# Null key and null value folded into keys and values by a context column, in a two-layer gated cross-attention kernel

## The reference

```python
x = layer_norm(x, g_norm)
q = x @ Wq
kv = context @ Wkv
k, v = jnp.split(kv, 2, axis=-1)
q, k, v = (to_heads(q), to_heads(k), to_heads(v))
nk = jnp.broadcast_to(null_kv[0], (b, HEADS, 1, DIM_HEAD))
nv = jnp.broadcast_to(null_kv[1], (b, HEADS, 1, DIM_HEAD))
k = jnp.concatenate([nk, k], axis=2)
v = jnp.concatenate([nv, v], axis=2)
...
attn = jax.nn.softmax(sim.astype(jnp.float32), axis=-1).astype(sim.dtype)
out = jnp.einsum('bhij,bhjd->bhid', attn, v)
out = out.transpose(0, 2, 1, 3).reshape(b, -1, INNER)
out = out @ Wout
return layer_norm(out, g_out)
```

## Time and profile before

| what | value |
|---|---|
| median of 3 runs | 330.18 us (328.82 to 331.27) |
| profiled execution | 329.04 us, of it 327.2 us span |
| TensorE busy (weight loads) | 92% (75%) |
| VectorE, ScalarE, GpSimd busy | 74%, 70%, 53% |

### The profile page before, as it was taken

One profiled execution on the slowest core, in us unless ns is written; L12 is line 12 of the kernel. 1 busy time (PEld: TensorE's weight loads), 2 busy tenths in 40 slices (PEclk: granted clock), 3 DMA queues, 4 the chain that ended last, 5 costly groups with the idle time before them and its releaser, 6 DMA issues.

```text
span 327.2 us, 7975 instructions
## 1 busy us (share of the span) xinstructions
PE 301.6 (92%) x2682; PEld 245.2 (75%) x2682; DVE 240.8 (74%) x723; ACT 230.5 (70%) x781; POOL 173.9 (53%) x301
## 2 busy tenths in 40 slices
PE   6779999999999869999999999999999998977595
PEld 6557668686767658898998988989888777743375
DVE  3887999999885456666777787777777686547865
ACT  2776596969899677877878778787787774319190
POOL 3115616252443145458889797895957849245100
PEclk9999999999999999999999999999999999979989
DMA  5671010002020000000000000000000000000004
GB/s 148 164 205 26 1 26 1 1 2 66 3 62 3 0 0 2 2 2 2 2 3 2 1 4 2 2 0 3 3 2 1 2 3 1 2 0 1 2 0 130
DMA packets 12649, 7.22 MB, mean 22 GB/s; under 512 B 3969, under 2 KB 12161, under 8 KB 12609
## 3 DMA queue, kind: packets, MB, share of 16 engines
q1 hardware_dynamic: 11728, 6.51, 7.2%
q10 hardware_dynamic: 880, 0.20, 0.3%
HBM read 5.66 MB, written 1.05 MB: 20 GB/s over the span
## 4 chain that ended last, share of the span: by engine, by line
PE 73%; DVE 8%; issue 7%; ACT 7%; POOL 4%; DVEq 0%; POOLq 0%; ACTq 0%
PE psum L1084 14%; PE psum L1220 10%; PE psum L1517 9%; PE psum L1531 7%; PE psum L1088 7%; PE psum L1090 6%; PE psum L1089 6%; PE psum L1099 2%; ACT work L1025 2%; DVE hgm L2149 2%; PE psum L1632 2%; PE psum L1540 1%; PE psum L1095 1%; DVE work L2008 1%; PE psum L1317 1%
## 5 line engine op out<-in xcount | busy, mean ns | idle before, releaser
L1025 ACT ACTIVATE work<-psum,nmx 128x129 f32<-128x129 f32 x256 | 83.4, 420 | 25.9 <-DVE nmx L2014 24.8
L603 POOL TENSOR_TENSOR work<-work,rden 128x512 f32<-128x512 f32 x64 | 66.4, 1038 | 0.0
L2014 DVE TENSOR_REDUCE nmx<-psum 128x4 f32<-128x516 f32 x64 | 41.5, 689 | 29.4 <-PE psum L1220 29.3
L1084 PE MATMUL psum<-ident,work 128*128 128x128 f32 (+2 forms) x376 | 58.4, 281 | 3.9 <-DVE work L2008 2.6
L1025 ACT ACTIVATION_READ_ACCUMULATOR work<-psum,nmx 128x1 f32 x256 | 58.7, 229 | 0.0
L1088 PE MATMUL psum<-split 128*128 128x256 f32 (+2 forms) x128 | 52.0, 406 | 1.5 <-issue 0.8
L1084 PEld LDWEIGHTS psum<-ident,work 128*128 128x128 f32 (+2 forms) x376 | 41.7, 142 | 13.1 <-issue 3.3
L2008 DVE COPY work<-psum 128x512 f32<-128x512 f32 x64 | 43.9, 686 | 7.8 <-PE psum L1084 4.9
L1090 PE MATMUL psum<-split 128*128 128x256 f32 (+2 forms) x128 | 43.3, 338 | 0.0
L1089 PE MATMUL psum<-split 128*128 128x256 f32 (+2 forms) x128 | 43.2, 338 | 0.0
L1220 PE MATMUL psum<-KT,work 64*128 64x129 f32 x512 | 37.5, 285 | 2.5 <-DVE den L2024 1.8
(11 more groups left out here) (209 smaller groups left out, 576.6 us busy)
## 6 DMA issues: line engine op xcount, KB each, us to landing
KT<-in_L_xattn_Wkv SPq DMA_DIRECT2D x2, 384.0 KB, 5.2
X<-in_x SPq DMA_DIRECT2D x1, 768.0 KB, 6.8
out_x<-X SPq DMA_DIRECT2D x3, 256.0 KB, 2.3
work<-in_ctx SPq DMA_DIRECT2D x3, 192.0 KB, 2.6
KT<-in_L_xattn_Wout SPq DMA_DIRECT2D x1, 512.0 KB, 4.7
work<-in_L_xattn_Wq SPq DMA_DIRECT2D x1, 512.0 KB, 3.6
work<-in_L_xattn_Wout SPq DMA_DIRECT2D x1, 512.0 KB, 4.0
X<-in_x SPq DMA_DIRECT2D x1, 256.0 KB, 3.3
```

Of the source, the lines that this page charges most:

```text
L603: pool.tensor_tensor(sx_[:, :, 0:S], sx_[:, :, 0:S], bcast(rden[n % 2][:, :], S), ALU.mult).then_inc(p_ready.sem, 1)
L1025: ins = act.activation(Sx[n % 4][:, j, :], psum[:, here, (j // 2) * K1:(j // 2 + 1) * K1], ACT.Exp, bias=nmx[n % 2][:, j:j + 1], accum_out ...
L1084: return pe.transpose(dst, src, ident[0:m, 0:m])
L2014: dve.tensor_reduce(nmx[n % 2][:, :].rearrange("p (c a) -> p c a", a=2), sim, AX_X, ALU.max, negate=True).then_inc(max_done.sem, 1)
```

## The change

The 97th column of the masked context is now minus the mask in place of the inverted mask, and the null value becomes a 97th row of the value weights, as the null key is one of the key weights. So an open position gets its key less the null key and its value less the null value, and a masked one gets zeros. Taking the null key off every key takes the same number off every logit of a row, so the softmax stays; the null logit is 0 and its key column is filled with zeros. The probabilities, the null one included, add up to 1, so the output is the product with the reduced values plus the null value, which ScalarE adds as a bias column while it copies the output (`oT`). What falls away: `pnr`, `pnT`, `nw`, `nvb`, the null transposes and products, their copies on ScalarE and VectorE and GpSimd's multiplication L601, the early load of the output weights (the later one, `ld_wo2`, stays) and the two loads of the null key as a column. There is one new small load, of 16 pieces of 256 bytes, in SP's queue right behind the value weights.

```diff
             load(wkv_f[1][0:CD, :], wkv[:, INNER:2 * INNER], ld_wv)
+            load(wkv_f[1][CD:CD + 1, :].rearrange("p (h e) -> p h e", h=NH),
+                 null_kv[1:2, :].rearrange("o (h e) -> o h e", h=1).to_broadcast([1, NH, DH]), ld_wv)
...
-            load(nk_col[0:DH, :], nk, ld_small)
-            load(nk_col[DH:P, :], nk, ld_small)
...
-            load(wo_f, wo_v, ld_wo)
...
-                pool.tensor_scalar(nvb, nvb, nv_col, None, ALU.mult).then_inc(setup_p.sem, 1)
...
-                pool.tensor_copy(KTb[:, :, :, S:K1].rearrange("p c b o -> p c (b o)"),
-                                 ones_of).then_inc(null_keys.sem, 1)
+                pool.memset(KTb[:, :, :, S:K1], 0.0).then_inc(null_keys.sem, 1)
...
-                pool.tensor_copy(cm_g[:, :, CD:CD + 1].rearrange("p b o -> p (b o)"),
-                                 not_mcol[:, s * G:(s + 1) * G]).then_inc(cm_done.sem, 1)
+                pool.tensor_scalar(cm_g[:, :, CD:CD + 1].rearrange("p b o -> p (b o)"), mcol[:, s * G:(s + 1) * G], -1.0,
+                                   None, ALU.mult).then_inc(cm_done.sem, 1)
...
-                if n % UPT < 2 and t >= 2:
-                    pool.wait_ge(pnt_done.sem, pnt_done.at(t - 1))
-                pool.tensor_tensor(pnr[t % 2][:, b % 2, HPU * hg:HPU * hg + HPU], sx_[:, :, S], rden[n % 2][:, :],
-                                   ALU.mult).then_inc(pnr_done.sem, 1)
...
-                act.activation(oT, bank[5], ACT.Copy).then_inc(ot_out.sem, 1)
...
-                act.activation(pnT[0:NH, :], bank[7][0:NH, 2 * S:4 * S], ACT.Copy).then_inc(pnt_out.sem, 1)
+                act.activation(oT, bank[5], ACT.Identity, bias=nv_col[:, 0:1]).then_inc(ot_out.sem, 1)
...
-                    ins = pe.matmul(bank[4][0:NH, 0:D], nvb[:, c, :], wo_f[:, c, :], start=(c == 0),
-                                    stop=(c == NCH - 1))
...
-                    ins = product3(dst, hi[0:CD, tk], lo[0:CD, tk], wkv_hi[0:CD, w], wkv_lo[0:CD, w])
+                    ins = product3(dst, hi[0:CD + 1, tk], lo[0:CD + 1, tk], wkv_hi[0:CD + 1, w], wkv_lo[0:CD + 1, w])
...
-                    ins = pe.matmul(bank[7][0:NH, (2 + bb) * S:(3 + bb) * S], pnr[t % 2][:, bb, :], ident[:, :],
-                                    start=False, stop=False, skip_group_check=True)
...
-                    ins = pe.matmul(bank[7][:, bb * D:(bb + 1) * D], pnT[:, bb * S:(bb + 1) * S], nw[:, :],
-                                    start=False, stop=False, skip_group_check=True)
...
-                dve.tensor_copy(nw[0:NH, :], bank[4][0:NH, 0:D]).then_inc(setup_v.sem, 1)
...
-                    dve.wait_ge(pnr_done.sem, pnr_done.at(n - 1))
```

More of the change, by code:

```diff
@@ L71, in flamingo_kernel @@
     I1P = NC1 * P
-    SMALL_LOADS = 10
+    SMALL_LOADS = 8
     W1_LOADS = 5
-    SETUP_V = 18
+    SETUP_V = 17
     ATT_SCALE = float(DH) ** -0.5
@@ L177, in flamingo_kernel @@
         oT = work.carve(4 * S)
-        pnT = work.carve(2 * S)
         yS = work.carve(2 * D).rearrange("p (b d) -> p b d", b=2)
@@ L261, in flamingo_kernel @@
         rden = [sb(f"rden{n}", [P, HPU]) for n in range(2)]
-        pnr = [sb(f"pnr{n}", [P, 2, NH]) for n in range(2)]
         sty, stx = (sb(n, [P, 2, 6]) for n in ("sty", "stx"))
@@ L280, in flamingo_kernel @@
         sig = signal
-        ld_mask, ld_bias, ld_small, ld_l0, ld_w0, ld_x0, ld_x, ld_wq, ld_wk, ld_wv, ld_w1, ld_wo = (
-            sig("ld_" + n) for n in ("mask", "bias", "small", "l0", "w0", "x0", "x", "wq", "wk", "wv", "w1", "wo"))
+        ld_mask, ld_bias, ld_small, ld_l0, ld_w0, ld_x0, ld_x, ld_wq, ld_wk, ld_wv, ld_w1 = (
+            sig("ld_" + n) for n in ("mask", "bias", "small", "l0", "w0", "x0", "x", "wq", "wk", "wv", "w1"))
         ctx_loaded = sig("ctx_loaded", 16, start=0)
@@ L712, in split_wkv @@
             def split_wkv(n):
-                rows = CD + 1 - n
+                rows = CD + 1
                 if n == 0:
@@ L1034, in _ @@
                     exponents(2 * (m - 1) + 1)
-                t = pair_at(m, PNT_AT)
-                if t is not None:
-                    pn_evac(t)
                 t = pair_at(m, Y_AT)
@@ L1131, in int8_transposes, with down_scale_out @@
                 ins.then_inc(setup_t.sem, 1)
[L1133 to L1141 removed]
+            def down_scale_out():
                 pe.wait_ge(setup_a.sem, setup_a.at(8))
@@ L1367, in _ @@
             kv(10)
-            null_values_out()
+            down_scale_out()
             text_proj(1)
@@ L1565, in _ @@
                     ins.then_inc(q_done.sem, 1)
-                t = pair_at(m, NULL_AT)
-                if t is not None:
-                    null_out(t)
                 if in_rounds(m - WO_LAG):
@@ L1574, in _ @@
                     out_proj(m - WO_LAG, 1)
-                t = pair_at(m, PNT_AT)
-                if t is not None:
-                    null_transposes(t)
                 if in_rounds(m - T_LAG):
@@ L1658, in split_wkv @@
             def split_wkv(n):
-                rows, cols = CD + 1 - n, slice(n * INNER, (n + 1) * INNER)
+                rows, cols = CD + 1, slice(n * INNER, (n + 1) * INNER)
                 dve.wait_ge(wkv_hi_done.sem, wkv_hi_done.at(n + 1))
```

66 lines of the change are left out of this document (11 added, 55 removed).

## The result

| | before | after |
|---|---|---|
| median | 330.73 us (4 runs, 328.82 to 331.57) | 320.87 us (4 runs, 319.21 to 325.35) |
| ratio, with its 95% interval | | 0.9687 (0.9642 to 0.9732) |
| profiled execution, span | 329.04, 327.2 us | 321.48, 319.6 us |

Three of the four times after lie between 319.21 and 321.48 us; the ratio leaves out the fourth, a disturbed run. The forecast was 321.8 us, in a range from 318.8 to 325.0 us.

A forecast was written before the change was run, and what follows sets the result against it. TensorE bounds the kernel (73% of the span), with a 2.80 us floor it doesn't set in each round's first piece. 3.7 + 2.1 + 0.6 + 2.0 = 8.4 us off 330.18 gives 321.8 us, range 318.8 to 325.0.

The forecast's parts named there:

- The null transposes: Attention rounds, TensorE's own piece: removing them saves their whole 0.53 us in seven rounds, 3.7 us.
- The null products: Attention rounds, first piece with a 2.80 us floor: removal saves 0.35 us in six full rounds, 2.1 us; the seventh nothing.
- the round with the collision: One traced round of 5.12 us, 0.28 over ordinary, where VectorE's normalisation took 1.09 us just after GpSimd's multiplication began.
- ScalarE's copy: Output copy in the rounds: the bias adds 0.07 us, bounds 0 and 0.14, covered by 0.78 us idle before the exponents.
- The end: After the last scores: GpSimd's multiplication 0.15 us and eighth null transposes 0.54 go, biased copy adds 0.07; together 0.6 us.
- The start: Before the text product: TensorE's waits, null products of the weights and a GpSimd step go; 2.0 us, bounds 0.97 and 2.9.
- the lower bound: For the start's gain: at least TensorE's two waits, for the masked context and for GpSimd's power, 0.97 us.
- Rival 1: Start gives nothing much: VectorE's chain or later weights hold the text product, TensorE's freed time becomes a wait; 323.3 us, chance 0.12.
- Rival 2: Attention rounds: GpSimd's long multiplication starts earlier and shuts out VectorE's normalisation, costing 5 x 0.28 us; 323.2 us, chance 0.08.
- Rival 3: Attention rounds: another loop holds the 4.84 us period, so only start and end count; 327.6 us, chance 0.06.
- Rival 4: Attention rounds: the granted clock falls to 1.2 GHz, two such rounds costing 9.7 us; 331.5 us, chance 0.04.

The follow-up runs named there:

- experiment 1: Changed kernel with two fp32 products of the null transposes' shape put back before the values in rounds 5, 9, ..., result unused; 324.04 us.
- experiment 2: Changed kernel with two unused fp32 products 128x128x128 put back before the first output products in rounds 6, 10, ...; 321.66 us.
- experiment 5: Changed kernel with ScalarE's output copy as a plain Copy again, leaving the null value out of the output; 320.50 us.
- experiment 6: Changed kernel with GpSimd's small 128x4 multiplication back ahead of the long one in all 64 units, result unused; 320.58 us.
- experiment 9: Changed kernel with the early output-weight load, eight weight products on TensorE and a 128x128 GpSimd multiplication put back, results unused; 320.72 us.
- experiment 4: Changed kernel with the early 512 KB output-weight load and eight fp32 products on those weights on TensorE put back, result unused; 321.88 us.
- experiment 3: Changed kernel with the early 512 KB load of the output weights back ahead of x in SP's queue, read by nobody; 319.92 us.
- experiment 10: Changed kernel with only a 128x128 GpSimd multiplication by a column put back ahead of the power of group 1; 319.46 us.
- experiment 7: Changed kernel with two one-column copies on VectorE ahead of the first normalisation of each pair, to start it later; 320.98 us.
- experiment 8: Changed kernel with 9 and 19 more clock-keeping products ahead of the two global maxima; 320.84 us median of 4 runs, ratio 0.9651.
- experiment 11: Changed kernel with the null value row's load moved behind the layer 0 weights and clock-keeping products at 45 and 39; 320.29 us median, ratio 0.9677.
- experiment 12: The kernel before, unchanged, run and profiled once more; 330.85 us.

## Why the prediction was right

**The null transposes (3.7 us).** Right, mechanism and size. Seven rounds went from 5.37 to 4.84 us, and experiment 1 brought 3.79 us back with TensorE's part alone.

**The null products (2.1 us).** Right: six rounds from 5.19 to 4.84, the seventh unchanged, and experiment 2 brings 0.36 us back six times and nothing the seventh time. Reading the period against the ordinary round, rather than adding up the 0.60 us of the removed matmuls, gave the number: six times 0.60 would have been 3.6 us. The sum leaves 6.24 less 3.8 less 2.1, about 0.3 us, and that is the round with the collision, which the forecast did not count as a gain.

**ScalarE's copy.** Its cover held. Its price, 91 ns, is over the 70 ns taken and under the bound of 140. A nearer row than the two tiles of half the width was there, and I overlooked it: the kernel before has an activation at 128x512 with a scale column, though it is another function (Silu):

```profile
L833 ACT ACTIVATE work<-psum,dqg 128x512 f32<-128x512 f32 x16 | 10.9, 685 | 0.5 <-PE psum L1340 0.4
```

685 ns against 597 for the plain copy points to a column operand's price at the right size. The Trainium skill has it too: in "ScalarE: Activation LUTs", the section "What ACT_TABLE_LOAD costs", each column operand of an activation adds about 93 ns whatever the length. The runs agree: 91 ns.

**The end (0.6 us).** Right at 0.67 us. Experiments 1, 5 and 6 give its three parts: null transposes 0.55 (taken 0.54), copy 0.09 (taken 0.07), GpSimd's multiplications 0.24 (taken 0.15), together 0.70. The last was read a little wrong: the prediction took one small multiplication as the last unit's, but it is the last unit but one's, and the one before it counts as well.

**The start (2.0 us).** Right in sum at 2.08, and the step that named the path, through VectorE's residual and ScalarE's copy, is what decided: the residual moved by 1.85 us and the text product by 2.37. Of the 2.37 us, 0.29 did not arrive at the first scores; the way between the two takes 82.2 to 82.5 us from profile to profile. But the reasons given for "some 2 us" were only partly right, and that the sum fits so well is partly luck. TensorE's waits of 0.56 and 0.41 us, which stood in the sum and as the lower bound, are not the cause: in experiment 9 they were absent with 1.0 us of loss still there, and in the second profile of before the 0.56 us was absent too. Counted from the scaling of the weights, VectorE's residual was 1.96 us later before than after. What held it was VectorE's wait for GpSimd's rstd, the second of these rows, which I had not read. The first is a subtraction that waits for ScalarE's copy of the transposed context:

```profile
25.57 0.69 DVE L1749 TENSOR_TENSOR split<-psum,split 97x512 fp32r<-97x512 f32 x1 [1.72 <-ACT split L784]
...
27.37 1.12 DVE L1873 TENSOR_SCALAR V<-X,mv,rstd 128x128 f32<-128x128 f32 x4 [1.10 <-POOL rstd L482]
```

The wait of 1.72 us ahead of it was 1.01 us after. TensorE's 0.56 us lies in that difference, and the 1.10 us behind it would have been longer by as much without it.

The context chain ended behind the weight chain's 14.90 us by 2.48 us in the profile before: 0.53 us of it are the eight products (experiment 4), about 0.6 the GpSimd step (L487 took 0.61 us at 24.16, and experiment 9 shows that such a step passes through whole), and the rest, about 1.3 us, the later context. That one is again two things, which the issues on SP's queue show, of before and of after:

```profile
10.98 1.24 SPq L394 DMA_DIRECT2D nk_col<-in_L_xattn_null_kv  x2
...
16.50 2.50 SPq L436 DMA_DIRECT2D work<-in_ctx  x1
```
```profile
14.77 0.71 SPq L427 DMA_DIRECT2D work<-in_ctx  x1
```

From the issue at 16.50 to the multiplication at 23.21 it was 6.71 us, and now it is 5.85 (14.77 to 20.62): 0.86 us come from the transfer and 1.73 from the earlier issue. The two small loads of the null key had taken 1.24 us of the queue by themselves. Of these 2.59 us only what stands above the other chain counts. The size of this last part was not tried alone: no run has the two null key loads back. Part by part these are readings, from one profile each; what is shown is that two chains end there and which one is later in which kernel.

**What was not foreseen: 1.39 us lost at the end.** The forecast let the last stretch stand as it was, with its clock. It varies by chance. After the same idle of 3.15 us the 20 products took 4.55 to 4.83 us in both profiles of before and in experiments 1 to 4, 9 and 10, 5.78 us in experiment 7, and 6.05 us after and in experiments 5 and 6. Only with the idle time filled, in experiments 8 and 11, did they take 3.16. The other terms gave 0.6 us more than forecast, and so the profiled execution after is 0.9 us above the 320.6 us that was worked out for it. No effect of the change on this clock is shown; but with two profiles of before, neither with 6.05 us, such an effect is not excluded either.

**The rivals.** Rival 1 (start gives little) fell by the 2.08 us, though its wait did come, as 0.94 us in front of the text product. Rival 2 fell: its collision is real (experiment 7), but the removal of GpSimd's multiplication did not bring it on, and putting it back (experiment 6) did not change a round. Rival 3 fell by the rounds. Rival 4 fell in the rounds of the profile after, where no period grew; the clock did act, but in the last stage, and in four other profiles, one of them of the kernel before, in a single interval at the loop's entry. Adding up the forecast's terms with what was measured, 6.24 + 2.08 + 0.67 - 1.39 = 7.6 us, is the difference of the profiled spans; the medians are 9.3 us apart from the 330.18 us of the forecast to 320.87, 9.9 us from the 330.73 us of the four runs beside it. Medians of kernels whose runs scatter over 2 to 3 us can't tell these apart. (The lower end of the range, summed as stated, is 318.7 and not 318.8 us, which changes nothing.)

**Could it be faster still?** Filling the idle time ahead of both maxima keeps the clock (experiments 8 and 11), with 54.5 us from the last scores to the end, where the changed kernel without more products had 54.9 to 57.4 us by chance. In medians the two lie at 320.84 and 320.29 against 320.87, with intervals that overlap fully. So the lost clock is shown to be avoidable on the timeline; a gain in the measured time is not shown.

## What to carry to other kernels

Price removed work of a pipelined loop by the period of a round that has it against one that hasn't: 0.61 us of matmuls was worth 0.54 us in one place, 0.36 us in another and nothing in a third. Where a start has two chains that meet, follow each back through every engine that works in order, and look for the wait of the one that comes last; the waits of the busiest engine are not the ones to add up. Compare such starts by the distance from an event at the head of each chain to the one in which both end, since landings of the first loads move everything by a microsecond from run to run.

## What the runs showed of the hardware

- The first weights land with a scatter. VectorE waited for them between nothing and 1.78 us, and the first scores of kernels with the changed kernel's start came between 112.47 and 114.06 us (after and experiments 1, 2, 5 to 8). The distance from text product to first scores was 82.2 to 82.5 us in all.
- A clock dip at the loop's entry comes in some executions: the third interval between scores was 4.97, 5.17, 5.22 and 5.38 us in four profiles (experiments 2, 4, 8 and 12) and 4.19 to 4.20 us in the others.
- Two DMAs of 256 bytes, each in 64 pieces of 4 bytes, took 1.24 us of the issuing queue, nearly three times the 0.43 us of the one load of 512 KB. The transfer of those 512 KB made the context land 1.0 us later in experiment 3.
- A matmul of 128x16 by 128x128 takes as long as one of 128x128 by 128x128: four of each kind took 0.61 us.
